# Twelve products of a constant tile ahead of the first turn, the identity sent second, first statistics by two tiles, latent weights in two transfers

## The chip, the core and the metric

The kernel runs on 1 core of one Trainium2 chip. The metric is device time in microseconds (us), the median over runs of the whole kernel. Its engines are named as in the profile: PE is TensorE (matmul; PEld its weight loads), DVE is VectorE, ACT is ScalarE, POOL is GpSimd, and SP is SyncE, which here only issues transfers.

## What is computed

A two-layer block on 1024 tokens of 256 features: each layer adds an attention and a mixture-of-experts feed-forward of the same normalised input to the residual. The change touches only how the first layer begins:

```python
def _layernorm(x, axis=-1, eps=1e-05):
    m = jnp.mean(x, axis=axis, keepdims=True)
    v = jnp.var(x, axis=axis, keepdims=True)
    return (x - m) / jnp.sqrt(v + eps)
...
x = L0_attn_hidden_states
xn = _layernorm(x, axis=-1)
x = x + _L0_attn_ref(xn, ...) + _L0_ffn_ref(xn, ...)
# in _L0_attn_ref: hidden_states @ q_a_w.T, hidden_states @ kv_a_w.T   (the latents)
# in _L0_ffn_ref:  x = w_norm * (xf * rsqrt(mean(xf * xf) + EPS));  x @ w_router;  x @ sw_gate, x @ sw_up
```

## The kernel before

The 1024 tokens are eight tiles of 128 tokens (NT = 8), each 128 partitions by 256 features; KD = 2 is the number of 128-row halves of the features. Every engine has its own program written out by hand in `nc.Block()`, and the programs meet only at semaphores. There is no scheduler: the order in the code is the order of each engine.

The start of the kernel, up to about 24 us, runs as follows.

- **SP** (L712 on) issues all loads on one queue: two transfers of x (two tiles each, semaphores `x_in[0]` and `x_in[1]`), the first 141 columns of `consts`, which hold the 128x128 identity (`cf_in`), the whole of `w_lat` (the weights of the latents, the router and the shared gate, 418 columns for each of the two feature halves, `proj_in`), the other two transfers of x, then `rows`, `consts_b`, `sw_up`, `sw_down` and the rest.
- **DVE** (`statistics`, `variance`, `inverse`, `normal`) takes the mean and variance of tiles 0 to 3 (L1323, L1328, L1331), waits for the square root from ACT (L975), takes the reciprocal (L1336) and writes the normalised tiles `xn` (L1340); then it does the same for tiles 4 to 7, with a few small steps for the second norm between. After that come the eight tiles `x2` of the feed-forward's input (L1369), and then the statistics of each latent tile as ACT hands it over (L1386, L1387, L1376), with the low parts of the transposed `x2` (L1381) between.
- **PE** waits for the identity and for `xn`, and transposes pairs of tiles (`turn(g, ...)`, L1916: four transposes each). `turn(0)` and `turn(1)` come first, then the latent products of tiles 0 and 1 (L1931; one 128x417 product for each half k, into bank 4 or 5), then `turn(2)` and `turn(3)`, then the latent products of tiles 2 to 7, each of tiles 4 to 7 followed by a turn of two `x2` tiles. Then comes the shared expert's `shared_up` (L1952). Every product of fp32 operands shows as two instructions on PE.
- **ACT** loads its table, takes the square roots (`deviation`, L975), copies the turned tiles (`turned_copy`, L981) and the latents (L995) out of the banks, and rounds pieces of `sw_up` (L1007) and the turned `x2` (L987).
- **POOL** clears `zeros` (L808) and the last rows of `hT` (L809), and scales the router's columns of `w_lat` (L811, `route_scaled`), on which the latent products wait.

The lines that set the order around the change on PE and on DVE are these:

```python
            pe.wait_ge(cf_in, 16)
            for g in range(2):
                turn(g, xn, xn_done)
            pe.wait_ge(route_scaled, 1)
...
            statistics(range(HALF))
            variance(0)
            inverse(0)
            for i in range(HALF):
                normal(i)
            statistics(range(HALF, NT))
```

Of the kernel before, what the change touches and what calls it, by code (L numbers as in the profile page):

```python
# [18 lines left out]
P = 128  # L19
# [4 lines left out]
KD = D // P  # L24
# [12 lines left out]
LATX = LATW + E0 + 1  # L37
SETS = 2
# [261 lines left out]
def program(nc, t, y):  # L300

    ctx = ExitStack()
    with ctx:
# [119 lines left out]
        lat = r2.take(NT, LATX)  # L423
        ids = r2.take_b(2, NT * TOPK0, E0)
# [190 lines left out]
        fill_mm, fill_out, step_mask, low_rank = (sem(n) for n in ("fill_mm", "fill_out", "step_mask", "low_rank"))  # L615
# [97 lines left out]
        def _(sp):  # L713
            x_t = t["x"].rearrange("(t p) d -> p t d", p=P)
            for i in range(4):
                sp.dma_start(acc[:, 2 * i:2 * i + 2, :], x_t[:, 2 * i:2 * i + 2, :]).then_inc(x_in[i], 16)
                if i == 1:
                    sp.dma_start(cf[:, 0:CF_FIRST], t["consts"][:, 0:CF_FIRST]).then_inc(cf_in, 16)
                    sp.dma_start(w_lat, t["w_lat"]).then_inc(proj_in, 16)
# [19 lines left out]
            sp.wait_ge(zero_set, 1)  # L739
# [67 lines left out]
        def _(pool):  # L807
            pool.memset(zeros, 0.0).then_inc(zero_set, 1)  # L808
            pool.memset(hT[:, NF - 1, :], 0.0).then_inc(zero_set, 1)  # L809
            pool.wait_ge(proj_in, 16)  # L810
            pool.tensor_tensor(w_lat[:, :, LATW:LATX], w_lat[:, :, LATW:LATX],  # L811
                               w_lat[:, :, LATX:LATX + 1].broadcast_to([P, KD, E0 + 1]), ALU.mult).then_inc(route_scaled, 1)
# [108 lines left out]
            pool.tensor_tensor(step_maskT, second_maskT, first_maskT, ALU.subtract).then_inc(step_mask, 1)  # L921
            for j in range(2):
                pool.tensor_tensor(am_first[j], am_step[j], first_maskT, ALU.mult).then_inc(low_rank, 1)
            pool.wait_ge(step_mask, 1)
            for j in range(2):
                pool.wait_ge(low_rank, j + 1)
                pool.tensor_tensor(am_step[j], am_step[j], step_maskT, ALU.mult).then_inc(low_rank, 1)
# [9 lines left out]
            pool.wait_ge(low_rank, 4)  # L937
# [33 lines left out]
        def _(act):  # L971
            def deviation(h):
                half = slice(h * HALF, (h + 1) * HALF)
                act.wait_ge(ln_var, h + 1)
                act.activation(sd[:, half], var[:, half], ACT.Sqrt).then_inc(ln_sd, 1)  # L975

            deviation(0)

# [13 lines left out]
            deviation(1)  # L992
# [52 lines left out]
            act.wait_ge(zero_set, 1)  # L1045
# [272 lines left out]
        def _(dve):  # L1318
# [6 lines left out]
            def variance(h):  # L1325
                for i in range(h * HALF, (h + 1) * HALF):
                    dve.wait_ge(ln_stats, i + 1)
                    dve.bn_aggr(mv[:, i, :], stats[:, i, :]).then_inc(ln_mv, 1)  # L1328
                dve.wait_ge(ln_mv, (h + 1) * HALF)
                half = slice(h * HALF, (h + 1) * HALF)  # L1330
                dve.tensor_scalar(var[:, half], mv[:, half, 1], 1e-5, None, ALU.add).then_inc(ln_var, 1)  # L1331
# [1123 lines left out]
```

## Time and profile before

| what | value |
|---|---|
| time, median of 3 runs | 676.48 us (676.19 to 676.9) |
| the profiled execution: span, first to last instruction | 675.4 us |
| what lies around the span, median less span | 1.1 us |
| mean granted TensorE clock | 0.999 |
| busy: PE / DVE / ACT / POOL | 654.9 / 500.7 / 417.7 / 298.5 us |
| first matmul starts | 6.94 us |
| first product of the shared expert (L1952) starts | 24.23 us |

The profile gives no whole time of the profiled execution beside its span; the difference to the median of the runs stands for what lies around it. Busy time counts an engine's own instructions; PE is busy 97% of the span, so what matters is not how busy it is but how long its instructions take and what the first ones wait for.

### The profile page before, as it was taken

How to read it: one execution, taken by the hardware profiler on the slowest of the kernel's cores; microseconds unless marked ns; L12 is line 12 of the kernel's file. 1: busy time of each engine (PE TensorE's matmuls, PEld its weight loads, DVE VectorE, ACT ScalarE, POOL GpSimd, SP SyncE). 2: the span in 40 equal slices, each digit the busy share in tenths (PEclk: the TensorE clock that was granted, in tenths of full speed). 3: DMA queues.
4: the chain of work that ended last, by engine and by line, in shares of the span. 5: the costliest groups of instructions: out<-in, count | busy, mean ns of one | idle time of the engine just before them, and what ended most of it. 6: DMA issues, size and time to landing. Idle time of an engine off the chain costs nothing.

```text
span 675.4 us, 13827 instructions
## 1 busy us (share of the span) xinstructions
PE 654.9 (97%) x4756; PEld 573.9 (85%) x4756; DVE 500.7 (74%) x1425; ACT 417.7 (62%) x1084; POOL 298.5 (44%) x301
## 2 busy tenths in 40 slices
PE   5999999999999999999999998999999999999998
PEld 3777888898988899888888865556899999999997
DVE  6797877878778787887698788899577745645444
ACT  3766158888888888888865689998554222222221
POOL 1584146546464646452344418999532800400000
PEclk9999999999999999999999999999999999999999
DMA  8903034535535353444560000301100000000000
GB/s 316 378 5 102 1 112 128 167 116 165 165 112 191 100 180 115 123 129 125 210 257 1 1 1 1 112 1 53 75 1 1 2 17 1 1 16 1 2 16 16
DMA packets 26725, 59.43 MB, mean 88 GB/s; under 512 B 3146, under 2 KB 12748, under 8 KB 26272
## 3 DMA queue, kind: packets, MB, share of 16 engines
q1 hardware_dynamic: 23584, 50.35, 22.0%
q0 software_dynamic: 3072, 8.20, 3.7%
q8 instruction: 39, 0.64, 0.4%
q14 instruction: 30, 0.25, 0.1%
HBM read 48.24 MB, written 10.49 MB: 87 GB/s over the span
## 4 chain that ended last, share of the span: by engine, by line
PE 78%; DVE 10%; ACT 6%; issue 3%; POOL 2%; DMA 0%; ACTq 0%; POOLq 0%; DVEq 0%
PE bank L2292 10%; PE bank L2057 8%; PE bank L1991 7%; PE bank L2048 6%; PE bank L2343 5%; PE bank L2317 5%; PE bank L2077 4%; PE bank L2153 4%; PE bank L2068 4%; PE bank L1998 4%; ACT sb L1214 3%; PE bank L2119 3%; PE bank L2200 3%; PE bank L2359 3%; PE bank L1931 2%
## 5 line engine op out<-in xcount | busy, mean ns | idle before, releaser
L1073 ACT ACTIVATE sb<-bank,sb 128x256 f32<-128x256 f32 x128 | 59.6, 472 | 38.7 <-DVE sb L1578 33.5
L1281 ACT ACTIVATE h_parts<-sb 128x256 fp32r<-128x256 f32 x56 | 23.4, 418 | 76.5 <-DVE sb L1836 45.7
L2057 PE MATMUL bank<-sb 128*128 128x256 f32 x256 | 66.2, 381 | 0.0
L1578 DVE TENSOR_REDUCE sb<-bank 128x2 f32<-128x512 f32 x64 | 43.7, 683 | 27.1 <-PE bank L2057 26.6
L2292 PE MATMUL bank<-rounded,b_lo 128*128 128x256 f32 x224 | 63.0, 281 | 0.0
L2292 PE MATMUL bank<-rounded,b_hi 128*128 128x256 f32 x224 | 63.0, 281 | 0.0
L2292 PE MATMUL bank<-am_lo,b_hi 128*128 128x256 f32 x224 | 62.9, 281 | 0.0
L840 POOL DMA_INDIRECT expert_out<-sb x32 | 33.1, 1034 | 58.0 <-DVE sb L1520 44.2
L1080 ACT ACTIVATE sb<-sb 128x256 f32<-128x256 f32 x128 | 57.8, 505 | 0.1
L1827 DVE TENSOR_TENSOR sb<-sb,bank 128x256 f32<-128x256 f32 x56 | 23.4, 419 | 44.6 <-ACT sb L1238 44.5
L1238 ACT ACTIVATE sb<-bank 128x256 f32<-128x256 f32 x56 | 21.4, 382 | 53.3 <-PE bank L2292 53.3
L834 POOL DMA_INDIRECT sb<-rows_x,sb x32 | 32.8, 1026 | 42.6 <-PE bank L1991 21.2
L1991 PEld LDWEIGHTS bank<-sb 128*128 128x128 f32 (+1 forms) x384 | 46.0, 186 | 5.7 <-DVE sb L1514 3.6
L1991 PE MATMUL bank<-sb 128*128 128x128 f32 (+1 forms) x384 | 49.3, 278 | 0.8 <-DVE sb L1514 0.8
L1589 DVE TENSOR_TENSOR pt_parts<-bank,pt_parts 128x512 fp32r<-128x512 f32 x64 | 43.8, 684 | 8.5 <-ACT pt_parts L1093 6.6
L1838 DVE TENSOR_TENSOR h_parts<-sb,h_parts 128x256 fp32r<-128x256 f32 x56 | 28.7, 512 | 27.9 <-ACT h_parts L1281 27.9
L2057 PEld LDWEIGHTS bank<-sb 128*128 128x128 f32 x256 | 45.2, 190 | 4.8
L1214 ACT ACTIVATE sb<-sb 128x128 f32<-128x128 f32 (+1 forms) x128 | 46.7, 444 | 0.1
L2077 PE MATMUL bank<-pt_parts,xt_parts 128*128 128x256 f32 x256 | 46.0, 302 | 0.0
L2048 PE MATMUL bank<-rounded 128*128 128x512 f32 x160 | 42.8, 399 | 0.2 <-ACT sb L1102 0.2
L2292 PEld LDWEIGHTS bank<-rounded,b_lo 128*128 128x128 f32 x224 | 42.2, 188 | 0.0
L2292 PEld LDWEIGHTS bank<-rounded,b_hi 128*128 128x128 f32 x224 | 42.2, 188 | 0.0
(321 smaller groups left out, 1950.0 us busy)
## 6 DMA issues: line engine op xcount, KB each, us to landing
sb<-in_w_gate_up SPq DMA_DIRECT2D x32, 368.0 KB
sb<-in_w_down SPq DMA_DIRECT2D x32, 256.0 KB
sb<-in_w_pair SPq DMA_DIRECT2D x8, 704.0 KB
expert_out<-sb SPq DMA_DIRECT2D x1, 4096.0 KB, 23.5
sb<-expert_out SPq DMA_DIRECT2D x8, 512.0 KB, 6.8
sb<-in_w SPq DMA_DIRECT2D x1, 1792.0 KB, 12.9
sb<-in_b SPq DMA_DIRECT2D x1, 1792.0 KB, 7.4
sb<-in_sw_up SPq DMA_DIRECT2D x1, 1536.0 KB, 9.3
```

Of the source, the lines that this page charges most:

```text
L1073: act.activation(probs[:, u % 4, q, :], bank[3 + u % 2][:, q * S:(q + 1) * S], ACT.Exp, scale=-1.0, bias=row_min[:, u % 4, q:q + 1], accum ...
L1080: ins = act.activation(probs[:, slot, q, :], probs[:, slot, q, :], ACT.Copy, scale=row_inv[:, slot, q:q + 1])
L1214: act.activation(probs1[:, n % 4, a:b], masked[:, n % 4, a:b], ACT.Exp, scale=-1.0, bias=row_min[:, n % 4, q:q + 1]).then_inc(bl_exp, 1)
L1578: dve.tensor_reduce(row_min[:, u % 4, :], bank[3 + u % 2][:, :].rearrange("p (q n) -> p q n", q=QT), AX.X, ALU.min).then_inc(at_min, 1)
L1589: dve.tensor_tensor(r(probs_lo[:, u % 2]), bank[5 + u % 2][:, :].rearrange("p (a b) -> p a b", a=QT), probs_hi[:, u % 2], ALU.subtract).th ...
L1991: mm = pe.matmul(bank[1][0:n, to:to + P], w_gu[s][:, k, a:a + n], xeT[s][:, k, :], start=(k == 0), stop=(k == KD - 1))
L2048: mm = pe.matmul(where[:, :], r(w[i][:, cols]), r(q[:, half]), start=(n == 0), stop=(n == len(terms) - 1))
L2057: mm = pe.matmul(bank[3 + u % 2][:, q * S:(q + 1) * S], qb[i][:, h, b * S + q * P:b * S + (q + 1) * P], keys[:, h, b * S:(b + 1) * S], sta ...
L2077: mm = pe.matmul(bank[2 + 5 * h][:, 0:S], r(v_parts[:, QT * b + k, :]), r(part[:, u % 2, k, :]), start=(n == 0), stop=(n == len(terms) - 1))
L2292: mm = pe.matmul(dst, lhs, rhs, start=False, stop=(n == len(terms) - 1), skip_group_check=True)
L2317: pe.matmul(dst, r(w[:, 2 * k + j, :]), r(x[:, k, :]), start=(i + j == 0), stop=False, skip_group_check=True)
L2343: mm = pe.matmul(bank[4 + k][:, h * CW:(h + 1) * CW], r(w[:, rows_]), r(x), start=(f + h + i == 0), stop=(f == NF1 - 1 and i == 2), skip_g ...
```

## The change

The change does four things at the start of the kernel.

1. POOL fills a tile `warm` (256 fp32 columns, read as 512 bf16 columns) with 1.0 before its other two fills, and PE multiplies it by itself twelve times into bank 6 before it waits for the identity. Nothing reads the result; `warm` lies where the latents of tile 0 are written later.
2. SP sends the identity second, between the first and the second transfer of x, instead of third.
3. DVE works the first four tiles in two groups of two: `PARTS` = (0, 2), (2, 4), (4, 8). The statistics of tiles 2 and 3 stand between the variance and the reciprocal of tiles 0 and 1.
4. `w_lat` goes in two transfers, one for each half k, with a semaphore each; POOL scales each half for itself, and PE's first latent product waits for each half where it needs it.

The waits that count these events are renumbered (`zero_set` by one, `ln_sd` and `ln_rstd` by the number of parts), and `step_mask` is folded into `low_rank` much later in the program; these lines are left out below.

```diff
@@ -35,6 +35,8 @@
 NF = -(-FS // P)
 FH = FS - (NF - 1) * P
 LATX = LATW + E0 + 1
+PARTS = ((0, 2), (2, 4), (4, 8))
+WARM_UPS = 12
 SETS = 2
 PLACES = 3
 NEXT, SOONER = 6, 5
@@ -421,6 +423,7 @@
 
         r2 = strip(region2)
         lat = r2.take(NT, LATX)
+        warm = Strip(region2, 0, CH // 2).take(CH // 2)
         ids = r2.take_b(2, NT * TOPK0, E0)
         w_lat = Strip(region2, NT * LATX, KD * (LATX + 1)).take(KD, LATX + 1)
         sw_up = r2.take(KD, 2 * NF * P)
@@ -714,9 +717,11 @@
             x_t = t["x"].rearrange("(t p) d -> p t d", p=P)
             for i in range(4):
                 sp.dma_start(acc[:, 2 * i:2 * i + 2, :], x_t[:, 2 * i:2 * i + 2, :]).then_inc(x_in[i], 16)
+                if i == 0:
+                    sp.dma_start(cf[:, 0:CF_FIRST], t["consts"][:, 0:CF_FIRST]).then_inc(cf_in, 16)
                 if i == 1:
-                    sp.dma_start(cf[:, 0:CF_FIRST], t["consts"][:, 0:CF_FIRST]).then_inc(cf_in, 16)
-                    sp.dma_start(w_lat, t["w_lat"]).then_inc(proj_in, 16)
+                    for k in range(KD):
+                        sp.dma_start(w_lat[:, k], t["w_lat"][:, k]).then_inc((proj_in, lat_in)[k], 16)
             sp.dma_start(rows, t["rows"]).then_inc(rows_in, 16)
             sp.dma_start(cb[:, :], t["consts_b"]).then_inc(shared_in, 16)
             sp.dma_start(sw_up, t["sw_up"]).then_inc(shared_in, 16)
@@ -805,11 +810,13 @@
 
         @block.gpsimd
         def _(pool):
+            pool.memset(warm, 1.0).then_inc(zero_set, 1)
             pool.memset(zeros, 0.0).then_inc(zero_set, 1)
             pool.memset(hT[:, NF - 1, :], 0.0).then_inc(zero_set, 1)
-            pool.wait_ge(proj_in, 16)
-            pool.tensor_tensor(w_lat[:, :, LATW:LATX], w_lat[:, :, LATW:LATX],
-                               w_lat[:, :, LATX:LATX + 1].broadcast_to([P, KD, E0 + 1]), ALU.mult).then_inc(route_scaled, 1)
+            for k in range(KD):
+                pool.wait_ge((proj_in, lat_in)[k], 16)
+                pool.tensor_tensor(w_lat[:, k, LATW:LATX], w_lat[:, k, LATW:LATX],
+                                   w_lat[:, k, LATX:LATX + 1].broadcast_to([P, E0 + 1]), ALU.mult).then_inc(route_scaled, 1)
             for n in range(SU_STEPS):
                 pool.wait_ge(w_high, n + 1)
                 pool.tensor_tensor(r(su_step(su_lo, n)), su_step(sw_up, n), su_step(su_hi, n), ALU.subtract).then_inc(w_low, 1)
...
@@ -970,11 +976,12 @@
         @block.scalar
         def _(act):
             def deviation(h):
-                half = slice(h * HALF, (h + 1) * HALF)
+                part = slice(*PARTS[h])
                 act.wait_ge(ln_var, h + 1)
-                act.activation(sd[:, half], var[:, half], ACT.Sqrt).then_inc(ln_sd, 1)
+                act.activation(sd[:, part], var[:, part], ACT.Sqrt).then_inc(ln_sd, 1)
 
             deviation(0)
+            deviation(1)
 
             def turned_copy(g, dst):
                 act.wait_ge(turned, g + 1)
@@ -989,7 +996,7 @@
 
             for g in range(2):
                 turned_copy(g, xnT)
-            deviation(1)
+            deviation(2)
             for i in range(NT):
                 act.wait_ge(lat_mm, i + 1)
                 act.activation(lat[:, i, :], bank[4 + i % 2][:, 0:LATX], ACT.Copy).then_inc(lat_out, 1)
@@ -1323,32 +1330,37 @@
                     dve.bn_stats(stats[:, i, :], acc[:, i, :]).then_inc(ln_stats, 1)
 
             def variance(h):
-                for i in range(h * HALF, (h + 1) * HALF):
+                part = slice(*PARTS[h])
+                for i in range(*PARTS[h]):
                     dve.wait_ge(ln_stats, i + 1)
                     dve.bn_aggr(mv[:, i, :], stats[:, i, :]).then_inc(ln_mv, 1)
-                dve.wait_ge(ln_mv, (h + 1) * HALF)
-                half = slice(h * HALF, (h + 1) * HALF)
-                dve.tensor_scalar(var[:, half], mv[:, half, 1], 1e-5, None, ALU.add).then_inc(ln_var, 1)
+                dve.wait_ge(ln_mv, PARTS[h][1])
+                dve.tensor_scalar(var[:, part], mv[:, part, 1], 1e-5, None, ALU.add).then_inc(ln_var, 1)
 
             def inverse(h):
-                half = slice(h * HALF, (h + 1) * HALF)
+                part = slice(*PARTS[h])
                 dve.wait_ge(ln_sd, h + 1)
-                dve.reciprocal(rstd[:, half], sd[:, half]).then_inc(ln_rstd, 1)
+                dve.reciprocal(rstd[:, part], sd[:, part]).then_inc(ln_rstd, 1)
+                dve.wait_ge(ln_rstd, h + 1)
 
             def normal(i):
-                dve.wait_ge(ln_rstd, i // HALF + 1)
                 dve.tensor_scalar(xn[:, i, :], acc[:, i, :], mv[:, i, 0:1], rstd[:, i:i + 1], ALU.subtract, ALU.mult)\
                     .then_inc(xn_done, 1)
 
-            statistics(range(HALF))
+            statistics(range(*PARTS[0]))
             variance(0)
+            statistics(range(*PARTS[1]))
             inverse(0)
-            for i in range(HALF):
-                normal(i)
-            statistics(range(HALF, NT))
+            normal(0)
+            normal(1)
             variance(1)
             inverse(1)
-            dve.wait_ge(ln_rstd, 2)
+            normal(2)
+            normal(3)
+            statistics(range(*PARTS[2]))
+            variance(2)
+            inverse(2)
+            dve.wait_ge(ln_rstd, len(PARTS))
             dve.tensor_tensor(ms, mv[:, :, 1], rstd, ALU.mult).then_inc(ms_step, 1)
             normal(4)
             dve.wait_ge(ms_step, 1)
@@ -1917,10 +1929,13 @@
                                           src[:, 2 * (g % 4) + i, k * P:(k + 1) * P], ident)
                 mm.then_inc(turned, 1)
 
+            pe.wait_ge(zero_set, 1)
+            for n in range(WARM_UPS):
+                warmb = warm.bitcast(BF16)
+                pe.matmul(bank[6][:, :], warmb[:, 0:P], warmb, start=True, stop=True)
             pe.wait_ge(cf_in, 16)
             for g in range(2):
                 turn(g, xn, xn_done)
-            pe.wait_ge(route_scaled, 1)
             for i in range(NT):
                 if i == 2:
                     for g in range(2, 4):
@@ -1928,6 +1943,8 @@
                 pe.wait_ge(turned_out, i // 2 + 1)
                 at_least(pe, lat_out, i - 1)
                 for k in range(KD):
+                    if i == 0:
+                        pe.wait_ge(route_scaled, k + 1)
                     mm = pe.matmul(bank[4 + i % 2][:, 0:LATX], xnT[:, k, i * P:(i + 1) * P], w_lat[:, k, 0:LATX],
                                    start=(k == 0), stop=(k == KD - 1))
                 mm.then_inc(lat_mm, 1)
```

The instruction order on PE, at the start of its program. L1916 and L1928 are the transposes of `turn`, L1931 and L1948 the latent products; in the changed program L1935 is the products of the constant tile. Before:

```order
L1908 UNCONDITIONAL_BRANCH
L1916 MATMUL bank<-sb 128x128 x8
L1931 MATMUL bank<-sb 128x417 x4
L1916 MATMUL bank<-sb 128x128 x8
L1931 MATMUL bank<-sb 128x417 x6
```

and with the change:

```order
L1920 UNCONDITIONAL_BRANCH
L1935 MATMUL bank<-sb 128x512 x12
L1928 MATMUL bank<-sb 128x128 x8
L1948 MATMUL bank<-sb 128x417 x4
L1928 MATMUL bank<-sb 128x128 x8
L1948 MATMUL bank<-sb 128x417 x6
```

Twelve products are added at the head; the rest of PE's order is the same.

The order on DVE, from its first instruction to the end of the eight normalised tiles (BN_STATS is the statistics, the first TENSOR_SCALAR after BN_AGGR the variance, TENSOR_SCALAR 128x256 a normalised tile). Before:

```order
L1323 BN_STATS sb<-sb 128x6 x4
L1328 BN_AGGR sb<-sb 128x2 x4
L1331 TENSOR_SCALAR sb<-sb 128x4
L1336 RECIPROCAL sb<-sb 128x4
L1340 TENSOR_SCALAR sb<-sb 128x256 x4
L1323 BN_STATS sb<-sb 128x6 x4
L1328 BN_AGGR sb<-sb 128x2 x4
```

and with the change:

```order
L1330 BN_STATS sb<-sb 128x6 x2
L1336 BN_AGGR sb<-sb 128x2 x2
L1338 TENSOR_SCALAR sb<-sb 128x2
L1330 BN_STATS sb<-sb 128x6 x2
L1343 RECIPROCAL sb<-sb 128x2
L1347 TENSOR_SCALAR sb<-sb 128x256 x2
L1336 BN_AGGR sb<-sb 128x2 x2
L1338 TENSOR_SCALAR sb<-sb 128x2
L1343 RECIPROCAL sb<-sb 128x2
L1347 TENSOR_SCALAR sb<-sb 128x256 x2
L1330 BN_STATS sb<-sb 128x6 x4
L1336 BN_AGGR sb<-sb 128x2 x4
```

The reciprocal and the two normalised tiles of the first pair now stand behind the statistics of the second pair, and so behind the second transfer of x.

The order of SP's transfers. Before:

```order
L716 DMA sb<-in_x 128x2x256 x2
L718 DMA sb<-in_consts 128x141
L719 DMA sb<-in_w_lat 128x836
L716 DMA sb<-in_x 128x2x256 x2
L720 DMA sb<-in_rows 128x768
```

and with the change:

```order
L719 DMA sb<-in_x 128x2x256
L721 DMA sb<-in_consts 128x141
L719 DMA sb<-in_x 128x2x256
L724 DMA sb<-in_w_lat 128x418 x2
L719 DMA sb<-in_x 128x2x256 x2
L725 DMA sb<-in_rows 128x768
```

The second transfer of x moves behind the identity, and the third and fourth move one issue later.

## Rows read from the trace of the kernel before

**Rows 1.** The page: busy time of each engine, and the chain's shares by engine.

```profile
PE 654.9 (97%) x4756; PEld 573.9 (85%) x4756; DVE 500.7 (74%) x1425; ACT 417.7 (62%) x1084; POOL 298.5 (44%) x301
PE 78%; DVE 10%; ACT 6%; issue 3%; POOL 2%; DMA 0%; ACTq 0%; POOLq 0%; DVEq 0%
```

**Rows 2.** Chain of waits, 0 to 30 us: start, length, what.

```profile
6.06 0.75 DVE sb L1340 x2
6.81 0.14 issue
6.94 1.94 PE bank L1916 x8
8.88 4.54 PE bank L1931 x8
13.43 0.87 PE bank L1916 x8
14.30 4.21 PE bank L1931 x12
```

**Rows 3.** Single instructions of L1931, window 8.8 to 12.0, then 12 to 13.3.

```profile
L1931 PE MATMUL bank<-sb x5: 655/902/1034, 8.8 to 11.7; 128*128 128x417 f32 x5
...
L1931 PE MATMUL bank<-sb x4: 511/514/655, 11.7 to 12.9; 128*128 128x417 f32 x4
```

**Rows 4.** Timeline of all engines, 3.5 to 14.3 us: start, length, engine, line.

```profile
3.58 1.50 DVE L1323 BATCH_NORM_STATS2 sb<-sb 128x6 f32<-128x256 f32 x4 [3.58 <-DMA sb<-in_x]
6.06 1.38 DVE L1340 TENSOR_SCALAR sb<-sb 128x256 f32<-128x256 f32 x4
7.64 0.30 POOL L811 TENSOR_TENSOR sb<-sb 128x66 f32<-128x66 f32 x1 [5.70 <-DMA sb<-in_w_lat]
8.29 1.48 DVE L1323 BATCH_NORM_STATS2 sb<-sb 128x6 f32<-128x256 f32 x4 [0.84 <-DMA sb<-in_x]
11.62 0.73 DVE L1340 TENSOR_SCALAR sb<-sb 128x256 f32<-128x256 f32 x2
12.85 3.26 DVE L1369 SCALAR_TENSOR_TENSOR sb<-sb 128x256 f32<-128x256 f32 x8
14.14 4.37 PE L1931 MATMUL bank<-sb 128*128 128x417 f32 x12
```

**Rows 5.** Timeline: what an added fill and an added product cost.

```profile
0.74 0.31 POOL L808 MEMSET sb<- 128x256 f32 x1 [0.29 <-POOLq L2448]
...
24.23 0.71 PE L1952 MATMUL bank<-xt_parts,su_hi 128*128 128x512 f32 x2
24.77 0.63 PE L1952 MATMUL bank<-pt_parts,su_hi 128*128 128x512 f32 x2
25.24 0.63 PE L1952 MATMUL bank<-xt_parts,su_lo 128*128 128x512 f32 x2
```

**Rows 6.** SP's issues in the timeline, and issue to landing of the identity and x.

```profile
1.75 0.46 SPq L718 DMA_DIRECT2D sb<-in_consts  x1
...
2.73 0.95 SPq L716 DMA_DIRECT2D sb<-in_x  x2
...
sb<-in_consts SPq DMA_DIRECT2D x1, 70.5 KB, 4.8
...
DMA to landing us min/median/max: 2.8/4.3/5.8
```

**Rows 7.** Stages of 0.25 us; the last columns are clock, DMA share, GB/s.

```profile
4.25:4.50 0.25, 0.00 (x0) 0.00 (x0) 0.25 (x2) 0.00 (x0) 0.00 (x0) 1.00 0.20 49
8.50:8.75 0.25, 0.25 (x2) 0.00 (x0) 0.25 (x2) 0.17 (x1) 0.00 (x0) 1.00 1.12 414
```

**Rows 8.** Timeline and waits (us, times, longest) behind tile 3's latents.

```profile
17.56 1.05 ACT L1007 ACTIVATE su_hi<-sb 128x1024 fp32r<-128x1024 f32 x1
...
DVE sb L1386 <- ACT sb L995: 3.2, 4, 1.2
...
57.19 0.30 PE L1959 MATMUL bank<-sb 128*128 128x128 f32 x1 [0.36 <-DVE rounded L1467]
```

More of the change, by code:

```diff
@@ L614, in program @@
         b13_split, am_split = sem("b13_split"), sem("am_split")
-        fill_mm, fill_out, step_mask, low_rank = (sem(n) for n in ("fill_mm", "fill_out", "step_mask", "low_rank"))
+        fill_mm, fill_out, low_rank, lat_in = (sem(n) for n in ("fill_mm", "fill_out", "low_rank", "lat_in"))
         bl_q, bl_bias, bl_s, bl_min, bl_exp, bl_inv, bl_t, bl_even, bl_odd, bl_v, bl_oT, bl_turn, bl_o = (
@@ L737, in _ @@
                 expert_down(s, s)
-            sp.wait_ge(zero_set, 1)
+            sp.wait_ge(zero_set, 2)
             sp.dma_start(res.rearrange("(r p) d -> p r d", p=P), along(zeros, (1, NT * TOPK0))).then_inc(rows_out_done, 16)
@@ L920, in _ @@
             pool.wait_ge(fill_out, 16)
-            pool.tensor_tensor(step_maskT, second_maskT, first_maskT, ALU.subtract).then_inc(step_mask, 1)
+            pool.tensor_tensor(step_maskT, second_maskT, first_maskT, ALU.subtract).then_inc(low_rank, 1)
             for j in range(2):
                 pool.tensor_tensor(am_first[j], am_step[j], first_maskT, ALU.mult).then_inc(low_rank, 1)
-            pool.wait_ge(step_mask, 1)
             for j in range(2):
-                pool.wait_ge(low_rank, j + 1)
+                pool.wait_ge(low_rank, j + 2)
                 pool.tensor_tensor(am_step[j], am_step[j], step_maskT, ALU.mult).then_inc(low_rank, 1)
@@ L936, in _ @@
                         .then_inc(b13_split, 1)
-            pool.wait_ge(low_rank, 4)
+            pool.wait_ge(low_rank, 5)
             def low_rank_parts(c, kinds=(0, 1)):
@@ L1044, in _ @@
                         .then_inc(acc_done, 1)
-            act.wait_ge(zero_set, 1)
+            act.wait_ge(zero_set, 2)
             act.activation(row_sum[:, 0, :], zeros[:, 0:QT], ACT.Exp)
@@ L1672, in scale_and_shift @@
             def scale_and_shift(i):
-                dve.wait_ge(ln_sd, i + 3)
+                dve.wait_ge(ln_sd, len(PARTS) + i + 1)
                 dve.reciprocal(rstd[:, i:i + 1], sd[:, i:i + 1]).then_inc(ln_rstd, 1)
-                dve.wait_ge(ln_rstd, i + 3)
+                dve.wait_ge(ln_rstd, len(PARTS) + i + 1)
                 dve.scalar_tensor_tensor(shift[:, i:i + 1], mv[:, i, 0:1], -1.0, rstd[:, i:i + 1], ALU.mult, ALU.mult)\
@@ L2110, in _ @@
                     pe.wait_ge(sh_act, 4 * NF - 2)
-                    pe.wait_ge(zero_set, 2)
+                    pe.wait_ge(zero_set, 3)
                     pe.wait_ge(sh_h, 2 * NF - 1)
```

## The prediction

> **What bounds the kernel now.** I read the page first, then the chain of waits, then the timeline of the first 25 us. The page says that PE is busy 97% of a span of 675.4 us and makes up 78% of the chain that ends last [rows 1]. So time that PE gets back at the start is kept, unless something else is late behind it. The chain shows how the start runs [rows 2]: the first transfer of x lands at 3.56 us, DVE makes the first two normalised tiles by 6.81, PE begins at 6.94, and from there the chain is PE's own work up to 24 us.
>
> PE's first work is slow. Eight transpose instructions take 1.94 us from 6.94, and eight of the same take 0.87 us from 13.43; eight latent instructions take 4.54 us from 8.88, and twelve take 4.21 us from 14.30, so eight would take 2.81 [rows 2]. Single latent products last up to 1034 ns before 12 us and 514 ns after [rows 3]. That is the engine at 1.2 GHz and then at 2.4 GHz; it had stood idle until 6.94 us, and rose at about 12.2 us. The clock column reads 1.00 in this stretch too [rows 7], so it doesn't show the slow stretch; the durations do. The slow clock costs (1.94 - 0.87) + (4.54 - 2.81) = 2.80 us. That is what the twelve products are after, and it is not what they can bring, as the steps show.
>
> **The change, part by part.**
>
> *The twelve products.* POOL's fill of 256 columns takes 0.31 us from 0.74 [rows 5], so PE starts at about 1.15 us. A 512-column product at full clock starts every 0.233 us (two in 0.47 us, from 24.77 to 25.24) [rows 5], at half clock 0.47 us. Twelve at half clock take 5.6 us and end at 6.75; if the clock rises on the way they end earlier, at 4.0 us at the very least. Bank 6 isn't needed by anybody before 12 us. POOL's other fills start 0.3 us later, hidden: nobody waits for them before 9 us.
>
> *The first pair of tiles.* The first statistics start at 3.58, one every 0.36 us. Two end at 4.29; from the end of four statistics (5.08) to the first normalised tile (6.06) pass 0.98 us [rows 4]: four aggregates, variance, square root on ACT, reciprocal. Two aggregates less are worth about 0.1, so 0.88 for a pair. I put the variance of the first pair at 4.72, half of that behind 4.29. Then DVE does the statistics of tiles 2 and 3, which need the second transfer of x. If it is there, they end at 5.45; the square root is done by then, the reciprocal ends at about 5.65, and two normalised tiles at 6.40 (two take 0.73 [rows 4]). PE, 0.14 us behind [rows 2], starts its first turn at 6.55 or when the twelve end, 6.75, against 6.94. The second pair then needs 0.88 + 0.73 = 1.6 us, is done at 8.0, and its turn starts at 8.15 and ends at 8.6 at full clock.
>
> *The latents of tiles 0 and 1.* Eight instructions at 0.35 us: 8.6 to 11.4, against 13.43 now. The weights don't hold them: the whole `w_lat` was there at 7.64 and was scaled in 0.30 us [rows 4]; the first half needs to be scaled by 8.6, the second 0.7 us later. The two pieces cost one more issue, 0.46 us on SP [rows 6], and one more POOL instruction of at most 0.3 us, hidden beside PE's second turn. That cover ends 0.6 us after 8.0; beyond it PE would wait for POOL, and still have the slack of the next step.
>
> *The third and fourth turn.* They need tiles 4 to 7. DVE can't start those before the third transfer of x has landed, 8.29 us, and with its work above done at 8.0 it waits for that transfer as before. The last two normalised tiles start at 11.62 and end at 12.35 [rows 4], and nothing in the change makes that earlier. So the fourth turn starts at 12.35 + 0.13 = 12.48, lasts four instructions of 0.109 us, and the latents of tile 2 start at 12.92 instead of 14.14 [rows 4]. **That is 1.22 us, the whole gain**: the other 1.6 us of the 2.80 turn into a wait of PE for DVE, which shows as idle time around 11.5 and 12.3.
>
> *Behind it.* After tile 3's latents ACT does 1.05 us of rounding and then copies tile 4's latents without a pause [rows 8]: all that moves along with PE. DVE is through its `x2` tiles at 16.1 as before [rows 4], which is now late for the statistics of the latents. But it idled for 3.2 us in four waits for them up to 24 us [rows 8], so it can take 1.2 us less and still catch up by the last tile. At 57.19 PE waits 0.36 us for DVE [rows 8], so from 24 to 57 us both are in the chain, and both have moved by the same amount. From there on the rest only shifts.
>
> *The transfers.* Two things are not in the trace. (a) The third transfer of x is issued one transfer later, 0.45 us [rows 6]. Between 0 (the engines are full around its landing: share 1.12 and 414 GB/s at 8.5 us [rows 7], so the order of bytes decides and the bytes ahead of it are the same) and 0.45 us. It is nearer to the first; I take 0.2. (b) The second transfer of x goes out 0.48 us later and behind the identity. It landed at about 4.3 us (issue to landing 2.8, then some 3.1 us [rows 6]). Now 4.8 if it keeps that pace. The identity itself took 4.8 us from its issue [rows 6], while the share of the transfer engines fell to 0.20 and 49 GB/s at 4.25 us, against 1.12 at 8.5 us [rows 7]: something was thin just there. If x has to follow such a transfer on the same queue, it lands at 1.22 + 4.8 = 6.0 plus up to 0.7. It costs nothing until 5.0 us, since DVE has 8.29 - 8.0 = 0.3 us to spare, and one for one after that. I take 4.8 and no cost, since x took 3.1 us with a transfer of four times the size ahead of it.
>
> The Trainium skill ("DMA: Bandwidth & Descriptors", Anatomy of one DMA) puts a transfer, measured for software-made descriptors, at about 2.0 us plus bytes over 436 GB/s. The 2.8 us of the first x agree (2.6 by the page), the identity's 4.8 us don't (2.2). By the page the third x would have landed before 8.0, and the sum would be 1.5 us; by the rows it is 1.22 less 0.2.
>
> **Sum.** 1.22 - 0.2 = 1.0 us. The span goes from 675.4 to 674.4, the time, 1.1 us above it, from 676.48 to 675.5. A measurement of this kernel tells 0.2%, 1.35 us, from no change; the forecast is inside that.
>
> **Rivals.**
>
> *More: the third x is not late and comes a little early.* DVE is ready at 8.0; were the third x there too, the gain would be 1.22 + 0.3 = 1.5 us, 675.0 us. For it: the low share around 4.25 us, which another order may fill. Against: the same bytes stand ahead of it. The rule of the Trainium skill above would give this case. This, or 1.35 us and more by any mixture, has 0.28.
>
> *No gain: the clock.* If the twelve products don't raise it, or it falls again before 8.6, when PE has only eight transposes in some 2 us, the start is as now: turns end at 9.1 instead of 8.88, the clock rises in the latents as before, and the time is 676.4 to 676.8. For it: PE's idle stretch between the twelve and the first latents. Against: it rose at 12.2, behind 5.3 us of work that began at 6.94, and the twelve are 5.6 us of work without a pause. It has slack, too: the latents may end at 12.0 instead of 11.4 before the fourth turn is late, so a rise up to about 9.8 us costs nothing. The Trainium skill ("TensorE: Matmul & The Clock Gate", Part 1) says that the engine is throttled by default, that activity lifts this, and that how many products run slow differs from run to run. No row here shows a second run. That the second x lands near 6.3 gives the same time: tiles 4 to 7 would start at 9.5 instead of 8.29, and the 1.2 us are gone. Together 0.14.
>
> *Slower: the second x is held by the identity.* With x at 6.8 us, its statistics end at 7.5, the first turn starts at 8.6, the second pair is done at 10.0, DVE reaches tile 4 then instead of at 8.29, and the latents of tile 2 start at 14.14 + 0.5: 677.0. If the clock has fallen in those two idle microseconds, the latents run slow again and it is 2.2 us over: 678.7. It decides from a landing at 6.3 us on. For it: the identity's 4.8 us. Against: the queue holds only 70.5 KB ahead of x. I give it 0.06 for being over by 1.35 us, and its milder half is counted above.
>
> **How the numbers follow.** The forecast (a gain of 0.5 to 1.35 us) has 0.52, the larger gain 0.28, no gain 0.14, slower 0.06. Faster by over 0.2% is the larger gain alone, 0.28; within 0.2% is 0.52 + 0.14 = 0.66; slower 0.06. The range leaves out the slower case and a tenth at the fast end: 674.7 (the 1.5 us and 0.3 for the spread of the runs, 676.19 to 676.9) to 677.0.
>
> **What would show it.** Right: PE's twelve products end by 6.75, the latents last 514 ns from the first, tiles 0 and 1's latents end near 11.4, PE idles before the third turn with DVE as its releaser, and L1952's first product starts near 23.2 instead of 24.23. Wrong: latents of 1034 ns (the clock); statistics of tile 2 later than 5.0 (the second x); tiles 4 to 7's statistics elsewhere than at 8.3 to 8.7 (the third x, either way); a DVE or ACT idle time between 17 and 57 us that is given back or grown.

## The result, and the profile after

| | before | after |
|---|---|---|
| time, median (21 runs each) | 677.13 us (676.19 to 678.48) | 678.28 us (676.63 to 680.45) |
| ratio, 95% interval | | 1.0016 (1.0009 to 1.0023) |
| profiled execution: span | 675.4 us | 676.7 us (its time: 678.53 us) |
| mean granted clock of it | 0.999 | 0.995 |
| end of the 12 products / first turn | none / 6.94 us | 5.19 / 7.57 us |
| second transfer of x lands | about 4.3 us | 5.81 us |
| tiles 0 and 1: eight latent instructions | 4.54 us | 4.80 us |
| first product of the shared expert | 24.23 us | 25.77 us |

The change makes the kernel 1.1 us slower, 0.16%, where 1.0 us less was forecast; the time is above the predicted range. The page of the changed kernel, busy time and the shares of the chain (they answer to [rows 1]):

```profile
span 676.7 us, 13857 instructions
...
PE 659.2 (97%) x4768; PEld 575.3 (85%) x4768; DVE 501.0 (74%) x1427; ACT 417.9 (62%) x1085; POOL 299.1 (44%) x303
...
PE 77%; DVE 10%; ACT 9%; issue 3%; DMA 1%; SPq 0%; POOL 0%; ACTq 0%; DVEq 0%
```

PE is busy 4.3 us longer than before, of which the twelve products are 4.1. The chain of waits of the changed kernel, start to 20 us (start, us, what), against [rows 2]:

```profile
0.74 0.44 SPq L719
...
1.24 0.45 SPq L721
...
1.75 4.06 DMA sb<-in_x
...
5.83 0.75 DVE sb L1330 x2
...
6.69 0.73 DVE sb L1347 x2
...
8.26 0.75 DVE sb L1347 x2
...
9.05 1.12 PE bank L1928 x4
10.17 4.80 PE bank L1948 x8
14.97 0.87 PE bank L1928 x8
15.85 4.21 PE bank L1948 x12
```

Before, the chain went through the first transfer of x. Now it goes through two issues (x, then the identity at L721) and the second transfer of x, which takes 4.06 us from its own issue at 1.75 and lands at 5.81. DVE then does the two statistics that it needs, and only behind them the reciprocal and the first normalised tiles. The timeline of the same stretch (start, us, engine, line, operation, what ended the idle time before it), against [rows 4]:

```profile
1.10 4.09 PE L1935 MATMUL bank<-sb 128*128 128x512 bf16 x12 [1.10 <-POOL sb L813]
3.54 0.75 DVE L1330 BATCH_NORM_STATS2 sb<-sb 128x6 f32<-128x256 f32 x2 [3.54 <-DMA sb<-in_x]
5.83 0.75 DVE L1330 BATCH_NORM_STATS2 sb<-sb 128x6 f32<-128x256 f32 x2 [1.12 <-DMA sb<-in_x]
7.57 1.09 PE L1928 MATMUL bank<-sb 128*128 128x128 f32 x4 [2.37 <-DVE sb L1347]
...
9.05 1.12 PE L1928 MATMUL bank<-sb 128*128 128x128 f32 x4 [0.40 <-DVE sb L1347]
9.96 5.01 PE L1948 MATMUL bank<-sb 128*128 128x417 f32 x8
14.81 1.03 PE L1928 MATMUL bank<-sb 128*128 128x128 f32 x8
15.68 4.37 PE L1948 MATMUL bank<-sb 128*128 128x417 f32 x12
```

The products start at 1.10 as forecast and end at 5.19; then PE stands idle for 2.37 us. The first turn takes 1.09 us for four instructions, so it runs at 1.2 GHz again, and so do the latents of tiles 0 and 1. The stretches of the changed kernel (stretch, length, busy time of PE, PEld, DVE, ACT and POOL, granted clock, share of the transfer engines, GB/s):

```profile
3.50:4.25 0.75, 0.75 (x4) 0.33 (x3) 0.71 (x3) 0.00 (x0) 0.00 (x0) 1.00 0.54 18
...
5.20:7.25 2.05, 0.00 (x0) 0.00 (x0) 1.38 (x5) 0.00 (x0) 0.14 (x1) 1.00 1.03 351
7.25:14.00 6.75, 6.03 (x14) 3.64 (x15) 5.44 (x28) 2.23 (x6) 0.51 (x2) 0.50 1.03 417
14.00:16.00 2.00, 2.00 (x12) 1.40 (x11) 2.00 (x6) 0.99 (x3) 0.00 (x0) 0.98 1.02 416
```

The granted clock is 0.50 from 7.25 to 14.0 us, which is 1.2 GHz: it fell after 2.05 us in which PE did nothing. Those 6.75 us at half make 3.4 of 676.7 us, the 0.005 that the mean clock of 0.995 lacks. The 21 runs sort by this: one with a mean of 1.0 took 676.63 us, twelve with 0.997 took 676.93 to 678.61, eight with 0.994 or 0.995 took 678.51 to 680.45. By their mean clock most runs were slow for a shorter time than the profiled one, and one not at all. Nothing after the shared expert's start is needed to explain the result: that start moved by 1.54 us, the span by 1.3.

The second transfer isn't the only slow one of the queue. The transfers issued behind it took from issue to landing (out, in, number, size of one, median us):

```profile
sb<-in_x SPq DMA_DIRECT2D x2, 256.0 KB, 5.3
sb<-in_w_lat SPq DMA_DIRECT2D x2, 209.0 KB, 4.8
```

So two causes offer themselves, and several theories on the first.

- **Order.** The second transfer of x, now third in the queue, lands 1.5 us later, and the turn waits for it.
- **Clock.** The products raise the clock, the wait of 2.37 us loses it, and the slow first stage is back.
- On the order, theory B says that the identity's short rows (70.5 KB) hold up what stands behind them; theory D says that whatever stands third in the queue is late.

In the expectations below, theory A is the clock.

### The profile page after: what moved, and what is told of

The parts are those of the page before. It is cut to its first block, busy times and chain, and to the rows that moved or that the text cites. A ratio compares the mean times of both kernels' runs of the same rounds, so it can differ in the third digit from the quotient of the medians.

```text
span 676.7 us, 13857 instructions
## 1 busy us (share of the span) xinstructions
PE 659.2 (97%) x4768; PEld 575.3 (85%) x4768; DVE 501.0 (74%) x1427; ACT 417.9 (62%) x1085; POOL 299.1 (44%) x303
## 4 chain that ended last, share of the span: by engine, by line
PE 77%; DVE 10%; ACT 9%; issue 3%; DMA 1%; SPq 0%; POOL 0%; ACTq 0%; DVEq 0%
PE bank L2309 10%; PE bank L2074 7%; PE bank L2008 6%; PE bank L2065 5%; PE bank L2360 5%; PE bank L2334 5%; ACT sb L1221 4%; PE bank L2170 4%; PE bank L2094 4%; PE bank L2015 4%; PE bank L2085 4%; PE bank L2136 3%; PE bank L2217 3%; PE bank L2376 3%; PE bank L2278 2%
```

## The experiments

Every experiment starts from the changed kernel unless said otherwise; each ratio is against the kernel before, run beside it on the same chip.

### e1: the change without its products

```diff
-WARM_UPS = 12
+WARM_UPS = 0
```

> The changed kernel without the twelve products; all else of the change stays. Theory A (the clock): the twelve raise the clock, but PE then idles from 5.2 to 7.57 us and the granted clock falls to 0.50 at 7.25, so they bring nothing; without them PE starts slow at 7.57 too, and the time is that of the changed kernel or up to 0.5 us less (1.16 us over before less 0 to 0.5). Rival B (the queue: x lands at 5.81 instead of about 4.3, whatever the clock does): the same, since the late start at 7.57 stays. Rival C (the products themselves disturb the start, by power or by bank 6): back to the kernel before, ratio 1.000. First turn at 7.57 in each.

678.72 us, 1.0022 (1.0013 to 1.0031). The second transfer of x took 3.95 us again and landed at 5.69. PE's timeline in e1:

```profile
7.45 1.08 PE L1928 MATMUL bank<-sb 128*128 128x128 f32 x4 [7.45 <-DVE sb L1347]
8.94 1.12 PE L1928 MATMUL bank<-sb 128*128 128x128 f32 x4 [0.40 <-DVE sb L1347]
9.84 3.66 PE L1948 MATMUL bank<-sb 128*128 128x417 f32 x8
```

The products don't make the loss, and they don't bring anything beside it: the difference to the change's 1.0016 lies inside the intervals. This profiled execution was its fastest (677.56 us, shared expert at 24.30), 1.2 us under its median, so it doesn't show where a median run loses its time. Here the clock rose within the latents, which take 3.66 us, earlier than in the changed kernel, where it stayed low until 14.0.

### e2: the products alone, in the kernel before

```diff
+        warm = Strip(region2, 0, CH // 2).take(CH // 2)
...
+            pool.memset(warm, 1.0).then_inc(zero_set, 1)
...
+            pe.wait_ge(zero_set, 1)
+            for n in range(WARM_UPS):
+                warmb = warm.bitcast(BF16)
+                pe.matmul(bank[6][:, :], warmb[:, 0:P], warmb, start=True, stop=True)
```

> The kernel before with the twelve products alone. PE idles only from 5.2 to 6.94 us. Theory A: if the clock is held over 1.7 us of idle time, the latents of tile 2 start at 12.9 instead of 14.14 and the time is 1.2 us under before; if it falls here too, the time is that of before within 0.3 us, and the latents last 0.9 to 1.03 us each again. Rival B: no gain and no loss from the clock; the time is that of before either way. Rival C: slower than before by about 1 us.

676.3 us, 0.9983 (0.9974 to 0.9992), shared expert at 22.80. PE's timeline in e2:

```profile
1.11 4.33 PE L1926 MATMUL bank<-sb 128*128 128x512 bf16 x12 [1.11 <-POOL sb L810]
6.90 1.21 PE L1919 MATMUL bank<-sb 128*128 128x128 f32 x8 [1.46 <-DVE sb L1343]
8.30 3.04 PE L1938 MATMUL bank<-sb 128*128 128x417 f32 x8 [0.19 <-ACT sb L984]
```

In this execution an idle stretch of 1.46 us leaves the clock up (ten of the eleven runs have a mean of 0.999 or 1.0, one has 0.997 and took 676.87): eight transposes in 1.21 us instead of 1.94, the latents in 3.04 instead of 4.54. Of those 2.2 us the kernel keeps 1.43, since the third transfer of x lands at 8.11 and the fourth turn can't start before 12.22. That is the ceiling that the prediction worked out.

### e3: 22 products, to cover the wait

```diff
-WARM_UPS = 12
+WARM_UPS = 22
```

> The changed kernel with 22 products instead of 12: they end near 7.4 us, just ahead of the first turn. Theory A: the clock stays at 1.00, turns take 0.44 us, the latents of tiles 0 and 1 take 2.8 us and end at 12.3, the last normalised tile (12.97) sets the fourth turn, and the latents of tile 2 start at 13.5 instead of 15.68: 2.1 us under the changed kernel, 0.6 to 1.0 under before. Rival B (only the late x): no more than 0.3 us better than the changed kernel.

676.92 us (676.65 to 677.36), 0.9993 (0.9984 to 1.0002), shared expert at 23.63. PE's timeline in e3:

```profile
1.10 6.61 PE L1935 MATMUL bank<-sb 128*128 128x512 bf16 x22 [1.10 <-POOL sb L813]
7.55 0.60 PE L1928 MATMUL bank<-sb 128*128 128x128 f32 x4
8.87 0.66 PE L1928 MATMUL bank<-sb 128*128 128x128 f32 x4 [0.72 <-DVE sb L1347]
9.36 2.97 PE L1948 MATMUL bank<-sb 128*128 128x417 f32 x8
```

The second x is late as in the change (its statistics start at 5.65), and ten more products take 0.0023 off the ratio (some 1.5 us) and 2.14 us off the shared expert's start. That is the clock's part, shown by itself: the first turn starts at 7.55 as in the change, 7.57. Without the idle stretch the eight latent instructions take 2.97 us instead of 5.01, and the runs lie close together.

### e4 and e11: the identity third again, the rest of the change kept

```diff
-                if i == 0:
+                if i == 1:
                     sp.dma_start(cf[:, 0:CF_FIRST], t["consts"][:, 0:CF_FIRST]).then_inc(cf_in, 16)
-                if i == 1:
                     for k in range(KD):
```

> The changed kernel with the identity sent third again, behind the second transfer of x. Rival B (the identity held x back): x's second transfer lands at 4.3 us again, the second pair is normalised at 8.0, the first turn starts at 6.6 to 6.9; time at least 0.7 us under the changed kernel. If instead the third transfer in the queue is the slow one whatever it is, the identity lands near 6.5 and x at 4.3: the same prediction for x. Theory A: PE idles 1.5 us instead of 2.4 behind the products; if that holds the clock, the time is 1.0 to 1.2 us under before, else it is that of before.

675.84 us, 0.9977 (0.9968 to 0.9986): ten runs from 675.68 to 676.05 and one of 677.5. The chain of waits and PE's timeline in e4:

```profile
0.74 2.76 DMA sb<-in_x
3.53 0.76 DVE sb L1329 x2
...
4.71 0.65 DVE sb L1329 x2
...
5.46 0.74 DVE sb L1346 x2
```

```profile
1.10 4.08 PE L1934 MATMUL bank<-sb 128*128 128x512 bf16 x12 [1.10 <-POOL sb L812]
6.34 0.63 PE L1927 MATMUL bank<-sb 128*128 128x128 f32 x4 [1.16 <-DVE sb L1346]
7.83 0.66 PE L1927 MATMUL bank<-sb 128*128 128x128 f32 x4 [0.86 <-DVE sb L1346]
8.32 2.97 PE L1947 MATMUL bank<-sb 128*128 128x417 f32 x8
```

One place in SP's order is worth 0.39% between the two ratios. The second x is there at 4.61 at the latest, the turn starts 1.23 us earlier than in the change, the idle stretch is 1.16 us instead of 2.37, and the clock holds. The third transfer of x is in by 7.68, so the slack behind it goes too: shared expert at 22.49. e11 is the same kernel again, on another chip:

> The kernel of e4 once more, beside the two others on the same chip: 1.6 us under before (0.9977 within 0.0009). The question is whether the two kernels that use ACT's queue are below it.

675.5 us, 0.9981 (0.9972 to 0.999), with ten runs from 675.01 to 675.75 and again one apart, 676.83. This is the best version of the study; the single run apart is not explained.

### e12: the identity second, and nothing else, in the kernel before

```diff
+                if i == 0:
+                    sp.dma_start(cf[:, 0:CF_FIRST], t["consts"][:, 0:CF_FIRST]).then_inc(cf_in, 16)
                 if i == 1:
-                    sp.dma_start(cf[:, 0:CF_FIRST], t["consts"][:, 0:CF_FIRST]).then_inc(cf_in, 16)
                     sp.dma_start(w_lat, t["w_lat"]).then_inc(proj_in, 16)
```

> The kernel before with the identity sent second and nothing else: no products, statistics by four, weights in one transfer. Theory D: x's second transfer lands 4 us behind its issue, near 5.8, the four statistics end at 6.55 instead of 5.08, the first normalised tiles come at 7.5, the first turn starts at 8.4 instead of 6.94, tiles 4 to 7 are reached at 9.0 instead of 8.3, and the time is 0.7 to 1.5 us over before. Rival: the loss of the changed kernel needs its pairs or its products; this kernel is then within 0.3 us of before.

678.41 us, 1.002 (1.001 to 1.003); the profiled execution took 679.24 us, its shared expert starts at 25.55. The chain of waits in e12:

```profile
1.74 4.57 DMA sb<-in_x
...
6.33 0.76 DVE sb L1324 x2
...
9.07 1.94 PE bank L1917 x8
11.01 3.74 PE bank L1932 x8
```

One swapped transfer makes a loss as large as that of the change (1.002 against 1.0016, each within 0.001). The first turn starts at 9.07 instead of 6.94, later than the 8.4 expected, since x landed at 6.31 and not at 5.8; the clock rises sooner in the latents (3.74 us instead of 4.54), which gives a part back.

### e7: another transfer of x in third place

```diff
-            for i in range(4):
+            for i in (0, 2, 1, 3):
```

(with the identity fourth, behind the transfers 0, 2 and 1 of x)

> The changed kernel with x's pairs sent in the order 0, 2, 1, 3 and the identity fourth: the pair that DVE waits for is third, behind an ordinary 256 KB transfer and not behind the identity. Theory D (the third transfer of the queue is slow, whatever it and the one ahead of it are): it lands about 4 us behind its issue, near 5.8, the first turn starts at 7.5, PE idles 2.3 us behind the products, and the time is that of the changed kernel, 1 us over before. Rival B (the identity's short rows held it): it lands 3.1 us behind its issue, near 4.8, the first turn starts before 6.8 (or when the identity is in, fourth in the queue), and the time is under before.

678.85 us, 1.0023 (1.0005 to 1.004), nine runs from 676.42 to 682.14, a wide spread; the run of 676.42 is the one whose mean clock is 1.0. The second x, third in the queue behind an ordinary transfer of 256 KB, took 4.22 us. PE's timeline in e7:

```profile
1.10 4.07 PE L1934 MATMUL bank<-sb 128*128 128x512 bf16 x12 [1.10 <-POOL sb L812]
7.73 1.08 PE L1927 MATMUL bank<-sb 128*128 128x128 f32 x4 [2.56 <-DVE sb L1346]
```

Theory B falls: nothing with short rows stands ahead, and x is as late, PE idles 2.56 us and the clock falls (0.50 from 7.25 to 14.0 as in the change). Theory D holds here and over the whole study, in a wider form: not the third alone, but the transfers from the third place on are slow. From issue to landing, by place in SP's queue, where all loads go on that queue:

| transfer | second in the queue, us | third, us |
|---|---|---|
| x, 256 KB | 3.1 (before, e7), 3.0 (e4) | 4.06 (after), 3.95 (e1), 3.9 (e3), 4.22 (e7), 4.57 (e12) |
| identity, 70.5 KB | 2.4 (after, e3, e12), 2.5 (e1) | 4.8 (before), 3.5 (e2), 3.9 (e4), 4.6 (e5), 5.0 (e6), 3.1 (e8), 3.8 (e11) |

Each row is late by its place: x by 0.8 us and more, the identity by 0.6 to 2.6. What comes behind is as late or later: in e4 the two halves of the weights, fourth and fifth, took 4.0 us each and the third x, sixth, 4.3; in the kernel before the third x, fifth, took 5.5. The first two places are the fast ones. Bytes ahead don't sort the rows: x in third place took 3.9 to 4.57 us with 326 KB ahead and 4.22 with 512 KB.

### e6: the identity third, without the products

e4 with `WARM_UPS = 0`.

> The kernel of e4 without the products: the earlier first turn and the two transfers of weights alone. Theory A: the first turn starts at 6.34 but at 1.2 GHz, turns take 1 us each, the latents of tiles 0 and 1 end between 12.5 and 14 us by when the clock rises, and the time is that of before, from 0.5 us under to 0.5 over: the order of the first tiles is worth nothing without the clock. Rival: the gain of e4 is DVE's and the transfers', the products add nothing to it: 1.2 us or more under before.

677.18 us, 0.9997 (0.9988 to 1.0006), against e4's 0.9977. The chain of waits in e6:

```profile
1.75 5.04 DMA sb<-in_consts
...
6.88 2.02 PE bank L1927 x8
8.90 4.45 PE bank L1947 x8
```

With the order put right, the products are worth 0.2%, while with the identity second they brought nothing clear (1.0016 against e1's 1.0022). Read the other way, the order is worth 0.25% without products and 0.39% with them. The gap between these two fits the lost clock, but lies within the intervals. Without the products the two-tile statistics, the split of `w_lat` and the rest bring nothing that the runs show. It also shows what stands on the other side of the order: here the identity took 5.04 us and landed at 6.79, and the turn waited for it until 6.88, though DVE had written its two tiles by 6.15.

### e8: the latent weights in one transfer

```diff
-                    for k in range(KD):
-                        sp.dma_start(w_lat[:, k], t["w_lat"][:, k]).then_inc((proj_in, lat_in)[k], 16)
+                    sp.dma_start(w_lat, t["w_lat"]).then_inc(proj_in, 16)
```

(from e4; POOL waits for `proj_in` for both halves)

> The kernel of e4 with the latent weights in one transfer again. In e4 tiles 4 and 5 were in by 7.68 us, when DVE came to them; before and in the kernel with the products alone they landed at 8.1 to 8.3. If the two transfers are what made them earlier, DVE starts tiles 4 to 7 at 8.1 to 8.3 here and the time is 0.4 to 0.6 us over e4. If not, the time is that of e4.

676.11 us, 0.9983 (0.9974 to 0.9992), the third x in by 7.63. Between this and e4 no difference shows (0.9983 and 0.9977, each within 0.0009): a cost or a saving of the split, one more issue ahead of the third x, would have to be smaller than that.

### e5: 17 products with the identity third

e4 with `WARM_UPS = 17`.

> The kernel of e4 (identity third) with 17 products, which then end near 6.3 us, just before the first turn at 6.34. In e4's profile PE already waits for DVE before the third turn, so the profile and the median should be those of e4 (1.6 us under before), within 0.2 us. If the one run of e4 in eleven that took 1.7 us more was one in which the clock fell between the products and the first turn, no run is more than 0.5 us above the median here; if it had another cause, such a run can come again. Rival: products beside DVE's and ACT's first steps slow them, and the time is over e4's.

676.2 us, 0.9985 (0.9976 to 0.9994), no better than twelve. The eleven runs lie between 675.75 and 676.86, with none apart, but spread wider than e4's other ten, so they don't tell what e4's single late run was. The first rows of PE's timeline in e5:

```profile
1.10 6.62 PE L1934 MATMUL bank<-sb 128*128 128x512 bf16 x17 [1.10 <-POOL sb L812]
7.55 1.04 PE L1927 MATMUL bank<-sb 128*128 128x128 f32 x8
```

Here the clock rose only at about 6.6 us: the products that start up to 6.2 us last 631 ns each, the last three 379. Seventeen took as long as e3's twenty-two, and the turn, ready at about 6.4, waited for them until 7.55. Products that run slow are a delay of their own: five more, one every 0.43 us, can add up to 2.1 us of wait by my estimate.

### e9 and e10: one transfer on ACT's queue

e9 is e4 with the identity issued by ACT ahead of its table load; e10 is the change with the second transfer of x issued there (and the identity still second on SP).

```diff
+            act.dma_start(cf[:, 0:CF_FIRST], t["consts"][:, 0:CF_FIRST]).then_inc(cf_in, 16)
```

> The kernel of e4 with the identity issued by ACT ahead of its table load instead of third by SP, so that the third transfer of SP's queue is a half of the latent weights, which nobody needs before 8 us. Theory D: the identity lands before 4.5 us, x's second transfer at 4.3 as in e4, and no transfer that PE or DVE waits for is third; the first turn starts at 6.3 to 6.4 in every run, set by DVE. The time is that of e4, or 0.2 us under it from the runs in which the identity would have landed later than 6.3. Rival: a transfer on ACT's queue takes from SP's first ones; tiles 0 and 1 come later than 3.6 us and the time is over e4's.

> The changed kernel (identity second on SP) with x's second transfer issued by ACT ahead of its table load. It undoes only the late landing. Theory D: x's second transfer lands by 4.4 us, the first turn starts near 6.4, PE idles 1.2 us behind the products instead of 2.4, the clock holds, and the time is that of e4, 2.4 us under the changed kernel. Rival (the order on SP costs in another way, by the third x or by the weights): it stays above before.

e9: 677.06 us, 1.0 (0.9991 to 1.0009), four runs at 675.79 to 675.87 and seven at 676.96 to 678.3. e10: 675.77 us, 0.9991 (0.9982 to 1.0001), though its median is 0.9982 of the one beside it, eight runs at 675.61 to 675.88, three at 676.95 to 678.55. In both profiles the first transfer of x, first on its own queue, landed at 4.1 us instead of 3.5, and e10's turn started at 6.89. On the second queue e10's x took 3.7 us from an issue at 0.74 and was in at 4.4, instead of 5.81 in the change; that alone, with the identity still second on SP, undoes the loss (0.9991 against 1.0016). But it takes 0.6 us from the first transfer. Both kernels fall into two groups some 1.2 us apart. Six of the ten runs in the slower groups have a mean clock of 0.996 or 0.997, none in the faster ones is below 0.999, so a lost clock is part of it; the profiles are of the faster groups, and what else the slower ones do stays open.

## Why the prediction was wrong

**The base.** The forecast counted from 676.48 us, the median of three runs. In 21 runs the same kernel took 677.13, which is already above the upper end of the range, 677.0. That is 0.65 of the 2.8 us between forecast and result; the other 2.15 are the step that follows, from 1.0 us less to 1.15 more.

**The second transfer of x: the step that failed.** "I take 4.8 and no cost, since x took 3.1 us with a transfer of four times the size ahead of it." It landed at 5.81. The range for it was right (4.8 to 6.7), and the identity's slow landing had been read, as a property of the identity. It was a property of the place, third instead of second, which the change gave to x. The reason offered, bytes ahead, is not what decides: e7's x had 512 KB ahead of it and took 4.22 us, e12's had 326 KB and took 4.57, and before it had 256 KB and took some 3.1. The Trainium skill ("DMA: Bandwidth & Descriptors", Anatomy of one DMA), whose fit for software-made descriptors is 2.0 us plus bytes over 436 GB/s, would give this transfer an estimated 2.6 us from its issue; the traces disagree with 3.9 to 4.57.

**What a late x costs.** The step allowed for a landing up to 5.0 us, "one for one after that". By that rule 5.81 costs 0.8 us and a small gain is left. The rule left out the clock: DVE's delay makes PE idle longer, and between an idle stretch of 1.46 us (e2, clock held) and one of 2.37 us (the change, clock lost) lie 1.8 us of latents, 3.04 against 4.80.

**The clock.** The rival had named PE's idle stretch "between the twelve and the first latents", but priced it at no gain, and treated the late x as an alternative to it ("that the second x lands near 6.3 gives the same time"). They are one mechanism: the late x is what makes the idle stretch long enough. The slower rival had both together, 2.2 us over, and set its point of decision at 6.3 us; 5.8 was enough. Its 0.06 was given for the identity's 4.8 us alone. The measured 1.15 us over lies between its two sizes, 0.5 and 2.2; that 678.28 comes so near its 678.7 is in part the luck of the low base.

**The twelve products.** "Twelve at half clock take 5.6 us and end at 6.75; if the clock rises on the way they end earlier, at 4.0 us at the very least." They ended at 5.19. That early end was read as harmless, but 1.5 us of cover were lost by it. The 0.47 us for one at half clock was too much, too: one starts every 0.43, and in e10 twelve that all last 634 ns end at 6.40.

**The ceiling.** "That is 1.22 us, the whole gain", set by DVE and the third x, was right in kind and size: e2, with the third x at 8.11, moved the shared expert by 1.43 us. In the change the term never came into play, since the latents ended at 14.97, behind the fourth turn's inputs.

**The third transfer of x.** Taken as 0.2 us later. In the change it landed at 8.3 us, as before, and DVE came to it only at 8.91, so the term counted for nothing. In e4, with one issue more ahead of it, it was in by 7.68, before DVE needed it; for the order of e4 the *More* rival was the better account: e4 stands 1.74 us ahead at the shared expert, against 1.5 forecast there.

**What lies around the span.** The 1.1 us were the difference between one profiled span and the median of other runs. Each run's own span and time give 2.25 us for the kernel before (median of the 33 runs beside e1 to e4) and 1.90 us for the change (21 runs). So the span grew by more than the time tells: the change's median span is 676.4 us, and the 677.13 us of the kernel before less 2.25 give an estimate of 674.9, so 1.5 us, of which 0.35 came back outside it.

**Behind 24 us.** Right: nothing there gave back or took anything. Over these profiles the span follows the start of the shared expert within 0.5 us: 22.49 and 673.8 (e4), 22.80 and 674.2 (e2), 23.63 and 675.0 (e3), 24.23 and 675.4 (before), 25.55 and 676.9 (e12), 25.77 and 676.7 (after).

Shown, then: the order makes the loss (e12 alone, e4 by undoing it, e10 by bringing x early in spite of it), its place in the queue and not the identity makes x late (e7), and the clock lost in the wait costs some 1.5 us, so that keeping it takes the loss away though x stays late (e3). Not shown: why the transfers from the third on land late. In the change the engines moved 18 GB/s between 3.50 and 4.25 us, 78 in e1 and 59 in e3, with at least six transfers issued, less than in any profile with x second (164 to 235 GB/s there, in before, e2, e4, e5, e6, e8 and e11); but e12 and e7, with x third and as late, moved 156 and 231, so the thin stretch alone isn't the cause either. The part of the two-tile statistics was not run by itself; e4 and e2, which differ by it and the split, lie within each other's intervals.

## What to carry to other kernels

A transfer that the first stage waits for should not give up its place in the queue to one that is needed later, even a small one: at the start of this kernel the place decided 0.8 us and more of each landing, and size and row length did not. Products that only raise the clock must reach up to the first real work, or nearly (in the profiles here 1.5 us of idle time kept the clock and 2.05 lost it, but one of e2's eleven runs has a lower mean clock), and whatever makes that work late takes their effect with it; but since they run slow in some executions, more of them than needed delays it too. Take the base from enough runs: three gave one 0.65 us too low. Take the time around the span from runs that give both numbers, not from one span and another run's time.

## What the runs showed of the hardware

- **The queue from its third transfer on.** The third took 3.1 to 5.0 us from issue to landing, in ten of twelve profiles 3.8 or more, against 2.4 to 3.1 for the two ahead of it, whatever it carries. The next ones were no faster (4.8 to 5.4 us for the fourth to seventh in the change). Cause open.
- **A lost clock comes back late.** In the change PE worked from 7.57 us on, and the granted clock stayed at 0.50 until 14.0; in e1, where it had never been raised, the latents that began at 9.84 were through in 3.66 us, partly at 2.4 GHz.
- **The clock column at the start.** It reads 1.00 from 0 us, also where twelve products of 512 columns take 5.21 us (e8) and transposes 0.27 us each (e1), so at the start it doesn't show the low level. The durations tell the clock there: a product lasts 634 ns at 1.2 GHz and 379 at 2.4.
- **The same products, two courses.** Twelve took 4.07 to 4.38 us in the change, e2, e4, e7 and e9, where the clock rose within them, and 5.2 to 5.3 in e8, e10 and e11, where all or nearly all of them last 634 ns. Even so the turn behind them ran at 2.4 GHz in e8 and e10 (four transposes in 0.60 and 0.63 us; 0.95 in e11). PE's first row in e8:

```profile
1.10 5.21 PE L1933 MATMUL bank<-sb 128*128 128x512 bf16 x12 [1.10 <-POOL sb L811]
6.14 0.60 PE L1926 MATMUL bank<-sb 128*128 128x128 f32 x4
```

- **Time around the span.** 2.18 to 2.38 us in all runs of the kernel before and of e12, 1.81 to 1.99 in all runs of the change and of e1 to e11, which have the fill of `warm` ahead of POOL's other two. So some 0.35 us of each of their gains, and of e2's 1.15 us too, lies outside the span and has nothing to do with the products (e1 and e6 have none and show it). That the fill is the cause was not tried by itself.
- **A second queue isn't free.** With one transfer on ACT's queue (e9, e10) the first transfer of x takes 3.3 to 3.4 us from its issue instead of 2.5 to 2.9, and in e10 the identity, second on SP, 3.4 instead of 2.4.
